# First feed-forward's slots: the low half of the second weight by a transfer inside SBUF instead of a GpSimd copy

## The chip, the cores and the metric

One core of a Trainium2 chip runs the whole program. The metric is the device time of one execution in microseconds (us); before the change it is 1437.46 us, the median of 3 runs (1436.73 to 1438.28). Engine names: PE is TensorE (PEld its weight loader), DVE is VectorE, ACT is ScalarE, POOL is GpSimd, SP is SyncE, which here only issues DMAs.

## The reference, cut to what matters

The program is four residual blocks on x of 16 x 256 tokens by 128: an attention, a feed-forward with experts, a second attention, a second feed-forward. The change is in the first feed-forward. Each token takes a shared expert and the 2 best of 8 experts (hidden width 512), weighted by a softmax over the two gate values:

```python
shared = silu(x_flat @ shared_w1.T) @ shared_w2.T
gate_logits = x_flat @ gate_w.T
top_k_gates, top_k_idx = jax.lax.top_k(gate_logits, TOP_K)
...
h = jnp.einsum('td,ehd->teh', x_flat, experts_w1)
expert_out = jnp.einsum('teh,edh->ted', jax.nn.silu(h), experts_w2)
selected = jnp.einsum('ted,te->td', expert_out, gates)
```

## The kernel before, in words

`first_ffn` does the shared expert for all tokens in 8 blocks of 512 and then the chosen experts in **39 slots** (`SLOTS`) of 256 tokens (`SLOT_T`). Tokens were scattered by expert into the DRAM table `xs`, each expert's stretch filled up to whole slots. So each slot has one expert, whose number is known only at run time: `table` holds, for each slot, the column at which that expert's weights begin.

Products are done in fp32r with each operand split in a high and a low part, hi·hi + hi·lo + lo·hi. A slot therefore needs four pieces of weights of 128 x 512 (256 KB each): high and low of w1, high and low of w2. They are copied into `ring`, which has two halves, used by even and odd slots. GpSimd makes all four copies: `take_w1` (L2199 high, rounded from w; L2200 low, from the table `w1l`) and `take_w2` (L2207 high, from w; L2210 low, from the table `w2l`). It reads the slot's column into a register with `value_load` first. `w2l` is filled beforehand by VectorE (`split_w2`, L2058), counted on `w_lo`.

The order on each engine is written out by hand, with semaphores between them. In round n:
- TensorE: turns x of slot n+1 into `ps_x` (`slot_in`), turns y of slot n-3 into `ps_t` (`slot_out`), `slot_up(n)` (L1846 to L1848, 12 products), `slot_down(n-1)` (L1860 to L1862, 12 products into the single `ps_y`; it waits for `w2_ready`, for `y_done` of the slot before and for `sl_done`).
- ScalarE: `xh` of slot n+1 (L1923), `yout` of slot n-3 from `ps_t` (L1969; `yout` has two buffers, so it waits for the store of two slots earlier, `stored`), then silu of slot n in two halves (L1929, into `s`), then its high part `sh` in two halves (L1980).
- VectorE: `xl` (L2109), the low part `sl` of slot n in two halves (L2143, `s` minus `sh`), then `yb`, the copy of `ps_y` of slot n-1 (L2135, signals `y_done`).
- GpSimd: w1 of slot n+1 once `slot_up(n-1)` is done, then w2 of slot n once `slot_down(n-2)` is done (`y_full`).
- SP, one queue in order: the load of x for slot n+4 into the three buffers of `xin` (L1757; waits until `slot_in(n+1)` is done, reads the slot's row into a register at L1756), then the store of slot n-3 from `yout` to `ys` (L1769; waits for L1969).

Of the kernel before, what the change touches and what calls it, by code (L numbers as in the profile page):

```python
# [16 lines left out]
F32 = mybir.dt.float32  # L17
# [22 lines left out]
SLOTS = (2 * B * S + EXPERTS * (SLOT_T - 1)) // SLOT_T  # L40
# [33 lines left out]
def wait(eng, sem, value):  # L74

    if not isinstance(value, int) or value > 0:
        eng.wait_ge(sem, value)
# [109 lines left out]
def scatter(nc, Z, rt, tile, xs, scattered, choices=(0, 1)):  # L187

    for k in choices:
        nc.gpsimd.indirect_dma_start(xs, bass.IndirectOffsetOnAxis(rt["at"][:, k, tile:tile + 1], 0),  # L190
                                     Z[:, tile * D:(tile + 1) * D], None).then_inc(scattered, 16)
# [1386 lines left out]
NT = B * S // TOK  # L1578
# [68 lines left out]
def first_ffn(nc, X, Z, ident, a):  # L1647
# [3 lines left out]
    E = 8  # L1651
    HC = 4
    HID = HC * P
# [11 lines left out]
    with ExitStack() as ctx:  # L1665
        def sb(name, shape, dt=F32):
            return ctx.enter_context(nc.sbuf_tensor("f0_" + name, shape, dt))
# [4 lines left out]
        def sem(name):  # L1672
            return ctx.enter_context(nc.semaphore("f0_" + name))
# [5 lines left out]
        ring = sb("ring", [P, 2, 4 * HID], F32R)  # L1679
# [12 lines left out]
        table, row_of = sb("table", [P, SLOTS], I32), sb("row_of", [P, SLOTS], I32)  # L1692
        pad_at = sb("pad_at", [P, EXPERTS], I32)
        w2l = sb("w2l", [P, E * HID], F32R)
# [23 lines left out]
        w_hi, w_lo, cast = sem("w_hi"), sem("w_lo"), sem("cast")  # L1718
        up_full, silu_done, sh_done, sl_done = sem("up_full"), sem("silu_done"), sem("sh_done"), sem("sl_done")
        y_half, y_full, y_done = sem("y_half"), sem("y_full"), sem("y_done")  # L1720
        t_full, t_done = sem("t_full"), sem("t_done")
        xin_loaded = [sem(f"xin_loaded{n}") for n in range(AHEAD)]
        stored = [sem(f"stored{n}") for n in range(2)]
        w1_ready, w2_ready = sem("w1_ready"), sem("w2_ready")
        block = ctx.enter_context(nc.Block(no_gpsimd_drain=True))

        def part(c2):
# [8 lines left out]
        w1h_at, w1l_at, w2h_at, w2l_at = [slice(n * HID, (n + 1) * HID) for n in range(4)]  # L1736

        @block.sync
        def _(sp):
            sp.wait_ge(zeroed, 1)  # L1740
            for n in range(SPARE):
                at = E * REGION + n * SLOT_T
                sp.dma_start(a["xs"][at:at + SLOT_T, :].rearrange("(t p) d -> p t d", p=P),
                             zero[:, :, :]).then_inc(padded, 16)
            sp.wait_ge(tables, TABLE)
            for e in range(E):
                at = nc.sync.value_load(pad_at[0:1, e:e + 1], min_val=e * REGION, max_val=e * REGION + B * S)
                sp.dma_start(a["xs"][bass.ds(at, SLOT_T), :].rearrange("(t p) d -> p t d", p=P),
                             zero[:, :, :]).then_inc(padded, 16)
            sp.wait_ge(padded, 16 * (SPARE + E))  # L1750
            sp.wait_ge(scattered, 16 * 2 * TILES)

            def load(n):
                if n >= AHEAD:
                    sp.wait_ge(x_full, NT + n - AHEAD + 1)
                at = nc.sync.value_load(row_of[0:1, n:n + 1], min_val=0, max_val=E * REGION + (SPARE - 1) * SLOT_T)  # L1756
                sp.dma_start(xin[:, n % AHEAD, :, :],  # L1757
                             a["xs"][bass.ds(at, SLOT_T), :].rearrange("(t p) d -> p t d", p=P)
                             ).then_inc(xin_loaded[n % AHEAD], 16)

            for n in range(AHEAD):
                load(n)
            for n in range(-1, SLOTS + BACK):
                if AHEAD <= n + AHEAD + 1 < SLOTS:
                    load(n + AHEAD + 1)
                if 0 <= n - BACK:
                    m = n - BACK
                    sp.wait_ge(t_done, NT + m + 1)
                    sp.dma_start(a["ys"][m * SLOT_T:(m + 1) * SLOT_T, :].rearrange("(t p) d -> p t d", p=P),  # L1769
                                 yout[:, m % 2, :, :]).then_inc(stored[m % 2], 16)  # L1770
            for n in range(2):
                sp.wait_ge(stored[n], 16 * ((SLOTS + 1 - n) // 2))

        @block.tensor
        def _(pe):
# [74 lines left out]

            def slot_down(n):
                pe.wait_ge(w2_ready, n + 1)
                wait(pe, y_done, NT + n)
                for c in range(HC):
                    if c % 2 == 0:
                        pe.wait_ge(sl_done, SHARED + 2 * n + c // 2 + 1)
                    hi, lo = [ring[:, n % 2, w.start + c * P:w.start + (c + 1) * P] for w in (w2h_at, w2l_at)]
                    o = n % 2 * 4 * SLOT_T + c * SLOT_T
                    cols, dst = slice(o, o + SLOT_T), ps_y[:, 0:SLOT_T]
                    nc.tensor.matmul(dst, hi, sh[:, cols], start=c == 0, stop=False)  # L1860
                    nc.tensor.matmul(dst, hi, sl[:, cols], start=False, stop=False)
                    last = nc.tensor.matmul(dst, lo, sh[:, cols], start=False, stop=c == HC - 1)  # L1862
                last.then_inc(y_full, 1)
# [292 lines left out]
        @block.gpsimd  # L2156
        def _(pool):
            nc.gpsimd.memset(zero[:, :, :], 0.0).then_inc(zeroed, 1)
            nc.gpsimd.memset(half[:, :], -0.5).then_inc(late_pool, 1)

            def rstd(n):

                pool.wait_ge(late_step, (LATE_Y_STATS, LATE_X_STATS)[n])
                nc.gpsimd.tensor_scalar(ve_late[:, :], mv_late[:, :, 1], EPS, None, ALU.add).then_inc(late_pool, 1)
                pool.wait_ge(late_pool, LATE_VE[n])
                nc.gpsimd.tensor_tensor(rs_late[:, :], ve_late[:, :], half[:, :], ALU.pow).then_inc(late_pool, 1)

            pool.wait_ge(scattered, EARLY)
            first = GROUPS[-2][0] * TPB
            scatter(nc, Z, rt, first, a["xs"], scattered, (0,))  # L2170
            rstd(0)
            scatter(nc, Z, rt, first, a["xs"], scattered, (1,))
            rstd(1)
            for i in range(first + 1, GROUPS[-1][0] * TPB):
                scatter(nc, Z, rt, i, a["xs"], scattered)
            def cast_into(n, w):
                nc.gpsimd.tensor_copy(w2l[:, n * HID:(n + 1) * HID], w[:, (n + 1) * HID:(n + 2) * HID]
                                      ).then_inc(cast, 1)

            for n in range(E):  # L2180
                cast_into(n, a["w1"])
            pool.wait_ge(routed, AT)
            for i in range(GROUPS[-1][0] * TPB, TILES):
                scatter(nc, Z, rt, i, a["xs"], scattered)
            for n in range(E):
                pool.wait_ge(w_lo, 2 + n + 1)
                cast_into(n, a["w2"])

            def expert_of(n):
                return nc.gpsimd.value_load(table[0:1, n:n + 1], min_val=0, max_val=(E - 1) * HID)  # L2190

            def take_w1(n, at):
                if n == 0:
                    pool.wait_ge(w_lo, 2 + E)
                elif n == 1:
                    pool.wait_ge(up_full, SHARED)
                else:
                    pool.wait_ge(up_full, SHARED + 2 * (n - 1))
                nc.gpsimd.tensor_copy(ring[:, n % 2, w1h_at], a["w1"][:, HID:][:, bass.ds(at, HID)])  # L2199
                nc.gpsimd.tensor_copy(ring[:, n % 2, w1l_at], w1l[:, bass.ds(at, HID)]).then_inc(w1_ready, 1)  # L2200

            def take_w2(n, at):
                if n == 1:
                    pool.wait_ge(y_full, NT)
                elif n > 1:
                    pool.wait_ge(y_full, NT + n - 1)
                nc.gpsimd.tensor_copy(ring[:, n % 2, w2h_at], a["w2"][:, HID:][:, bass.ds(at, HID)])  # L2207
                if n == 0:
                    pool.wait_ge(w_lo, 2 + 2 * E)
                nc.gpsimd.tensor_copy(ring[:, n % 2, w2l_at], w2l[:, bass.ds(at, HID)]).then_inc(w2_ready, 1)  # L2210

            pool.wait_ge(tables, TABLE)
            at = expert_of(0)
            take_w1(0, at)
            for n in range(SLOTS):
                if n + 1 < SLOTS:
                    after = expert_of(n + 1)
                    take_w1(n + 1, after)
                take_w2(n, at)
                at = after  # L2220
# [517 lines left out]
```

## Time and profile before

| what | value |
| --- | --- |
| median of 3 runs | 1437.46 us (1436.73 to 1438.28) |
| profiled execution | 1439.35 us |
| its span, first to last instruction | 1437.6 us |
| mean granted TensorE clock | 0.962 of full speed |
| PE busy | 1299.2 us (90%) |
| DVE busy | 1086.6 us (76%) |
| ACT busy | 971.9 us (68%) |
| POOL busy | 745.1 us (52%) |
| the slots | from about 583 to 715 us of the span |
| L2210, the copy that the change removes | 39 times, 612 to 1071 ns, median 617 |

Busy times are of the one profiled execution. A matmul's end is modelled, so PE's busy time says that the engine had work, not that it ran at its peak. Idle time of an engine matters only where something on the path to the end waits for it. In the rows below, a bracket such as [1.59 <-ACT f_sh L1980] says how long the engine had been idle before the instruction and what ended that; "issue" means that nothing in the profile explains it.

### The profile page before, as it was taken

Reading aid. Unit: us, or ns where it says so; the run is one execution under the profiler, and the core shown is the slowest. Engines: PE = TensorE matmul, PEld = TensorE weight load, DVE = VectorE, ACT = ScalarE, POOL = GpSimd, SP = SyncE. Lnnn points to the kernel's source line nnn. Section 1 sums busy time; section 2 is a strip of 40 time slices with the busy share of each in tenths; the row PEclk is TensorE's granted clock in tenths of the full one; section 3 lists DMA queues with packets and bytes.
Section 4 is the critical chain, followed back from the end, with each engine's and each line's share of the span. In section 5 each row is a group of like instructions: output and inputs, shape, how many; then the busy total and the mean of one; then the engine's idle time right before and its main releaser. Section 6 shows DMA issues by size and latency. Waiting matters only on the chain. (4 is left out here: it accounts for less than half of the span.)

```text
span 1437.6 us, 34171 instructions
## 1 busy us (share of the span) xinstructions
PE 1299.2 (90%) x12121; PEld 989.2 (69%) x12121; DVE 1086.6 (76%) x3011; ACT 971.9 (68%) x1499; POOL 745.1 (52%) x981
## 2 busy tenths in 40 slices
PE   2899999999999779999828999999999998799996
PEld 2456666666665467899826777777777776688886
DVE  5578888888877669566567898889888776476776
ACT  1588888888888546888714777777777777344341
POOL 4776666688764365788575554555454330101112
PEclk9799999999999889999958999999999999899999
DMA  6000000111111110222222111111111110225253
GB/s 238 17 23 20 22 21 20 26 31 31 29 31 46 36 60 27 64 74 79 60 80 59 49 48 48 47 47 48 48 47 39 40 40 17 60 61 133 67 133 82
DMA packets 84429, 77.20 MB, mean 54 GB/s; under 512 B 18224, under 2 KB 72240, under 8 KB 83888
## 3 DMA queue, kind: packets, MB, share of 16 engines
q1 hardware_dynamic: 80176, 66.73, 17.5%
q0 software_dynamic: 4096, 8.40, 2.0%
q8 instruction: 95, 1.56, 0.5%
q14 instruction: 62, 0.51, 0.1%
HBM read 36.26 MB, written 13.63 MB: 35 GB/s over the span
## 5 line engine op out<-in xcount | busy, mean ns | idle before, releaser
L545 ACT ACTIVATE a_p<-a_ps_s 128x1024 f32<-128x1024 f32 x256 | 258.3, 1030 | 21.9 <-PE a_ps_s L404 21.5
L1318 DVE TENSOR_REDUCE a_qt<-a_ps_d 128x2 fp32r<-128x512 f32 x256 | 174.9, 690 | 43.3 <-PE a_ps_d L1097 37.6
L655 DVE TENSOR_REDUCE a_qt<-a_ps_d 128x2 fp32r<-128x512 f32 x256 | 174.6, 688 | 39.9 <-PE a_ps_d L415 38.2
L827 POOL TENSOR_TENSOR a_rn<-a_ss,a_half 128x16 f32<-128x16 f32 x56 | 162.9, 2925 | 1.3
L1219 ACT ACTIVATE a_pg<-a_ps_s 128x1024 f32<-128x1024 f32 x128 | 125.8, 1024 | 24.1 <-PE a_ps_s L1086 22.5
L422 PE MATMUL a_ps_o<-a_p,a_v 128*32 128x256 f32 x2048 | 127.4, 388 | 3.8 <-ACT a_p L545 3.8
L1097 PE MATMUL a_ps_d<-a_kpad,a_qs 128*128 128x512 f32 x256 | 126.9, 499 | 3.6 <-DVE a_qt L1318 1.2
L415 PE MATMUL a_ps_d<-a_kpad,a_qs 128*128 128x512 f32 x256 | 126.7, 495 | 1.9 <-DVE a_qt L655 1.4
L2419 ACT ACTIVATE f_s<-f_ps_g 128x512 f32<-128x512 f32 x72 | 43.0, 599 | 99.2 <-PE f_ps_g L2355 99.0
L1506 POOL DMA_INDIRECT a_picked<-ys,rows x64 | 67.3, 1052 | 61.5 <-PE a_ps_d L1097 50.6
L2143 DVE TENSOR_TENSOR f_sl<-f_s,f_sh 128x512 fp32r<-128x512 f32 x78 | 59.3, 799 | 51.3 <-ACT f_sh L1980 51.2
L422 PEld LDWEIGHTS a_ps_o<-a_p,a_v 128*32 128x32 f32 x2048 | 60.4, 110 | 52.0 <-issue 20.6
L190 POOL DMA_INDIRECT xs<-Z,r_at x64 | 70.1, 1095 | 21.3 <-issue 15.2
L1075 PE MATMUL a_ps_a<-ident,a_qt 128*128 128x128 f32 x512 | 77.8, 275 | 1.4 <-ACT a_kc L1237 0.8
L1241 ACT CAST a_qsm<-a_ps_a 128x512 fp32r<-128x512 f32 x64 | 37.6, 587 | 58.1 <-PE a_ps_a L1075 58.1
L415 PEld LDWEIGHTS a_ps_d<-a_kpad,a_qs 128*128 128x128 f32 x256 | 48.2, 188 | 37.8 <-issue 10.7
L2512 DVE TENSOR_TENSOR f_h<-f_s,f_ps_u 128x512 f32<-128x512 f32 x72 | 48.7, 685 | 33.6 <-PE f_ps_y L2340 19.6
L2340 PEld LDWEIGHTS f_ps_y<-wd,f_p 128*128 128x128 f32 x512 | 63.8, 191 | 10.3 <-DVE f_p L2499 7.2
L2340 PE MATMUL f_ps_y<-wd,f_p 128*128 128x128 f32 x512 | 67.4, 278 | 3.3 <-DVE f_p L2499 2.8
L1147 PE MATMUL a_ps_o<-a_pg,a_v 128*32 128x256 f32 x1024 | 68.5, 385 | 0.4 <-ACT a_pw L1245 0.4
L1097 PEld LDWEIGHTS a_ps_d<-a_kpad,a_qs 128*128 128x128 f32 x256 | 48.5, 191 | 29.0 <-issue 11.4
L1245 ACT ACTIVATE a_pw<-a_ps_s 128x1024 f32<-128x1024 f32 x64 | 65.9, 1030 | 0.1
(385 smaller groups left out, 3790.8 us busy)
## 6 DMA issues: line engine op xcount, KB each, us to landing
a_kpad<-a_kc SPq DMA_DIRECT2D x512, 32.0 KB
f_gb<-spread SPq DMA_DIRECT2D x64, 256.0 KB, 5.6
a_kpad<-a_kq SPq DMA_DIRECT2D x256, 32.0 KB, 1.8
f_xin<-xs SPq DMA_DIRECT2D x39, 128.0 KB, 2.1
ys<-f_yout SPq DMA_DIRECT2D x39, 128.0 KB, 2.1
w<-in_w SPq DMA_DIRECT2D x2, 2304.0 KB, 11.3
out_x<-X SPq DMA_DIRECT2D x8, 256.0 KB, 6.6
xs<-f_zero SPq DMA_DIRECT2D x15, 128.0 KB, 1.9
```

Of the source, the lines that this page charges most:

```text
L190: nc.gpsimd.indirect_dma_start(xs, bass.IndirectOffsetOnAxis(rt["at"][:, k, tile:tile + 1], 0), Z[:, tile * D:(tile + 1) * D], None).then_ ...
L415: nc.tensor.matmul(bank(st.k, f"m{part}")[:, :], qs2[:, (st.k - 1) % 2, t * P:(t + 1) * P], kpad[:, u % PAD_RING, 2 * c:2 * c + 2, :].rear ...
L422: last = nc.tensor.matmul(ps_o[SLOT * j:SLOT * (j + 1), half * S:(half + 1) * S], v32[:, u % V_RING, t, j, :], probs[:, u % 2, j, t, :], s ...
L545: nc.scalar.activation(probs[:, u % 2, 2 * c:2 * c + 2, :, :].rearrange("p a b c -> p (a b c)"), ps_s[:, 2 * c:2 * c + 2, :].rearrange("p ...
L655: nc.vector.tensor_reduce(qt2[:, (k - PEAK) % 4, 2 * part:2 * part + 2, SHIFT], bank(k, f"m{part}")[:, :].rearrange("p (a b) -> p a b", b= ...
L827: nc.gpsimd.tensor_tensor(rn[:, part * c:(part + 1) * c], ss[:, part * c:(part + 1) * c], half[:, 0:c], ALU.pow).then_inc(rn_ready, 1)
L1075: last = nc.tensor.transpose(ps_a[:, n:n + P], stacked(src[:, (u // NG) % 2, kind, t * H + t0:t * H + t0 + G, :]), ident[:, :])
L1097: nc.tensor.matmul(bank(k, f"m{part}")[:, :], qs[:, k % 2, t * P:(t + 1) * P], kpad[:, k % PAD_RING, GLOBAL, 2 * c:2 * c + 2, :].rearrange ...
L1147: nc.tensor.matmul(ps_o[SLOT * j:SLOT * (j + 1), 0:S], v32[:, u % V_RING, t, j, :], pg[:, u % 2, j, t, :], start=t == 0, stop=t == TPB - 1)
L1219: nc.scalar.activation(pg[:, u % 2, 2 * c:2 * c + 2, :, :].rearrange("p a b c -> p (a b c)"), ps_s[:, 2 * c:2 * c + 2, :].rearrange("p a b ...
L1318: nc.vector.tensor_reduce(qt[:, b % 2, GLOBAL, n:n + 2, SHIFT], bank(k, f"m{part}")[:, :].rearrange("p (j s) -> p j s", s=S), AX.X, ALU.ma ...
L2340: last = nc.tensor.matmul(ps_y[:, t * D:(t + 1) * D], src, a["wd"][:, q * D:(q + 1) * D], start=q == 0 and t == 0, stop=q == NQ - 1 and t ...
```

## The change

One of the four pieces changes hands, the low part of w2: the copy L2210 is gone from GpSimd, and SP issues a DMA from `w2l` to `ring` for each slot, inside SBUF, with the column read into a register of SP. `w2_ready` is now signalled by the copy of the high part, and TensorE waits for the transfer as well, on a pair of semaphores used in turn. In SP's loop the new step stands ahead of the load and the store. For slot 0 it waits until `w2l` is complete, for slot n until `slot_down(n-2)` is done, as the GpSimd copy did.

```diff
+        w2l_loaded = [sem(f"w2l_loaded{n}") for n in range(2)]
...
+            def low_w2(n):
+                if n == 0:
+                    sp.wait_ge(w_lo, 2 + 2 * E)
+                else:
+                    sp.wait_ge(y_full, NT + n - 1)
+                at = nc.sync.value_load(table[0:1, n:n + 1], min_val=0, max_val=(E - 1) * HID)
+                sp.dma_start(ring[:, n % 2, w2l_at].bitcast(F32), w2l[:, bass.ds(at, HID)].bitcast(F32)
+                             ).then_inc(w2l_loaded[n % 2], 16)
+
             for n in range(AHEAD):
                 load(n)
             for n in range(-1, SLOTS + BACK):
+                if n + 1 < SLOTS:
+                    low_w2(n + 1)
                 if AHEAD <= n + AHEAD + 1 < SLOTS:
                     load(n + AHEAD + 1)
                 if 0 <= n - BACK:
...
             def slot_down(n):
                 pe.wait_ge(w2_ready, n + 1)
+                pe.wait_ge(w2l_loaded[n % 2], 16 * (n // 2 + 1))
...
-                nc.gpsimd.tensor_copy(ring[:, n % 2, w2h_at], a["w2"][:, HID:][:, bass.ds(at, HID)])
-                if n == 0:
-                    pool.wait_ge(w_lo, 2 + 2 * E)
-                nc.gpsimd.tensor_copy(ring[:, n % 2, w2l_at], w2l[:, bass.ds(at, HID)]).then_inc(w2_ready, 1)
+                nc.gpsimd.tensor_copy(ring[:, n % 2, w2h_at], a["w2"][:, HID:][:, bass.ds(at, HID)]
+                                      ).then_inc(w2_ready, 1)
```

## Rows read from the trace of the kernel before

**Rows 1.** Windows, mid-slots: stretch, length, PE PEld DVE ACT POOL busy, PEclk, DMA share, GB/s.

```profile
620.00:640.00 20.00, 19.90 (x165) 19.38 (x164) 12.77 (x24) 16.69 (x36) 16.77 (x24) 1.00 0.28 81
```

**Rows 2.** Waits, 565 to 720 us: waiter, what ended it, total us, times, longest.

```profile
PEld f_ps_y L1860 <- issue: 6.8, 20, 1.6
```

**Rows 3.** Timeline of PEld, starts of rounds and of `slot_down`: start us, duration us.

```profile
621.30 0.24 PEld L1778 LDWEIGHTS f_ps_x<-ident,f_xin 128*128 128x128 f32 x2
...
623.44 0.19 PEld L1860 LDWEIGHTS f_ps_y<-f_sh,f_ring 128*128 128x128 f32 x1 [0.20 <-issue]
...
624.88 0.24 PEld L1778 LDWEIGHTS f_ps_x<-ident,f_xin 128*128 128x128 f32 x2
...
626.73 0.19 PEld L1860 LDWEIGHTS f_ps_y<-f_sh,f_ring 128*128 128x128 f32 x1
...
628.19 0.24 PEld L1778 LDWEIGHTS f_ps_x<-ident,f_xin 128*128 128x128 f32 x2
```

**Rows 4.** Timeline of DVE in the same two rounds.

```profile
621.30 0.71 DVE L2143 TENSOR_TENSOR f_sl<-f_s,f_sh 128x512 fp32r<-128x512 f32 x1 [1.59 <-ACT f_sh L1980]
621.94 1.09 DVE L2143 TENSOR_TENSOR f_sl<-f_s,f_sh 128x512 fp32r<-128x512 f32 x1
622.96 0.41 DVE L2135 COPY f_yb<-f_ps_y 128x256 f32<-128x256 f32 x1
...
624.62 0.71 DVE L2143 TENSOR_TENSOR f_sl<-f_s,f_sh 128x512 fp32r<-128x512 f32 x1 [0.92 <-ACT f_sh L1980]
...
625.85 0.41 DVE L2135 COPY f_yb<-f_ps_y 128x256 f32<-128x256 f32 x1
```

**Rows 5.** Timeline of POOL, the copies of w2 in the same rounds.

```profile
621.73 0.77 POOL L2207 CAST f_ring<-w 128x512 fp32r x1 [0.25 <-PE f_ps_y L1862]
622.44 1.07 POOL L2210 CAST f_ring<-f_w2l 128x512 fp32r x1
...
625.30 1.11 POOL L2207 CAST f_ring<-w 128x512 fp32r x1 [0.51 <-PE f_ps_y L1862]
```

**Rows 6.** Timeline of ACT in the same rounds.

```profile
621.82 0.37 ACT L1923 CAST f_xh<-f_ps_x 128x256 fp32r<-128x256 f32 x1
622.09 0.38 ACT L1969 COPY f_yout<-f_ps_t 128x256 f32<-128x256 f32 x1
622.76 0.60 ACT L1929 ACTIVATE f_s<-f_ps_u 128x512 f32<-128x512 f32 x1 [0.29 <-PE f_ps_u L1848]
623.48 0.60 ACT L1929 ACTIVATE f_s<-f_ps_u 128x512 f32<-128x512 f32 x1
...
625.40 0.37 ACT L1923 CAST f_xh<-f_ps_x 128x256 fp32r<-128x256 f32 x1 [0.29 <-PE f_ps_x L1778]
```

**Rows 7.** Timeline of SP's queue: the first loads back to back, then mid-slots.

```profile
549.83 0.41 SPq L1757 DMA_DIRECT2D f_xin<-xs  x1
551.01 0.39 SPq L1757 DMA_DIRECT2D f_xin<-xs  x1
...
622.51 0.38 SPq L1757 DMA_DIRECT2D f_xin<-xs  x1
622.94 0.47 SPq L1769 DMA_DIRECT2D ys<-f_yout  x1
...
626.09 0.38 SPq L1757 DMA_DIRECT2D f_xin<-xs  x1
```

**Rows 8.** DMA issues (count, KB each, us to landing); then L1769's landings, and L1051's issues in ns.

```profile
f_gb<-spread SPq DMA_DIRECT2D x64, 256.0 KB, 5.6
ys<-f_yout SPq DMA_DIRECT2D x39, 128.0 KB, 2.1
X<-in_x SPq DMA_DIRECT2D x1, 256.0 KB, 2.8
...
DMA to landing us min/median/max: 1.8/2.1/4.1
...
L1051 SPq DMA_DIRECT2D a_kpad<-a_kc x512: 507/591/1687, 753.1 to 1198.6; - x171
```

## The prediction

> **What bounds the kernel now.** I first cut out the stretch in which the 39 slots run, because the change touches nothing outside it. In that view TensorE is busy 19.90 of 20 us at the full granted clock, GpSimd 16.77 and the DMA engines 0.28 of their time [rows 1]. So nothing on GpSimd or in a queue can save more than TensorE's few idle moments. The waits of the stretch say how few: TensorE's weight loader stood 6.8 us in front of L1860, the first product of `slot_down`, 20 times [rows 2]. That is the ceiling of any gain here.
>
> Next I read two rounds instruction by instruction. A round n of TensorE is: turn x of slot n+1, turn y of slot n-3, `slot_up(n)`, `slot_down(n-1)`. I call its start T. Rounds start at 621.30, 624.88 and 628.19 [rows 3]: one of 3.58, one of 3.31 us, and so in turn, 3.445 in the mean. The long one holds the gap at L1860 (0.20 us idle), the short one has none [rows 3]. TensorE is itself the bound in the short one.
>
> The long round is made by VectorE. The first half of `sl` starts at T+0.00 and takes 0.71, the second takes 1.09, then ps_y is copied to yb, 622.96 + 0.41 = 623.37, and TensorE goes on at 623.44 [rows 3, 4]. In the short round `sl` starts at T-0.26 and yb starts 1.23 us after it instead of 1.66 [rows 4]. The missing 0.43 us is GpSimd's: its copy of the **high** half of w2 (L2207) starts at 621.73, between the two halves of `sl`, and holds `sl`'s second half up until it ends at 622.50. The copy of the **low** half (L2210), which the change takes away, comes after that. It is the one that is held: 1.07 us, from 622.44 to 623.51, while VectorE runs [rows 5]. L2207 always starts 0.42 to 0.43 us after T, when the last `slot_down` is seen done, and after idle time of GpSimd [rows 5]; it is not late because of L2210.
>
> **The change part by part.**
>
> *39 copies L2210 leave GpSimd.* Some 0.6 us each when alone, 1.07 when held. They sit on no path: GpSimd idles 0.25 to 0.51 us before each L2207 as it is. w2 of slot n is copied from T of round n and needed in round n+1, and what gives way to whom stays (L2207 against the second `sl`). I take 0. Bounds: 0, or, if L2210 after all is what VectorE loses to, all long rounds become 3.31 (first rival).
>
> The Trainium skill (SBUF — State Buffer, section "Who interferes with whom") says that a VectorE instruction with two SBUF inputs and a GpSimd instruction that reads SBUF shut each other out for the whole instruction. The trace agrees (1.09 beside 0.71, 1.07 for the held copy); read alone, the rule speaks for this change, since a third less GpSimd reading should mean fewer clashes. Who starts first says which clash goes, and that one costs VectorE nothing.
>
> *One more wait on TensorE in `slot_down`.* It stands beside three others that are already passed in short rounds without a gap [rows 3], so 0 if the data is there. The transfer is issued at T+1.12 (below). It moves 256 KB from 128 rows of 2 KB; X's first load has that size and landed in 2.8 us, `f_gb`, of that size too but issued eight in a row, in 5.6 [rows 8]. With 2.8 it lands at T+3.9. `slot_down` of that slot starts in the next round, at T+3.445+1.85 = T+5.3 at the earliest. Slack 1.4 us; I take 0. If 5.6 it is 1.4 late, the third rival.
>
> *The SP queue.* This is where I expect the cost. SP runs in order. Now, in one pass, it waits for x turned, reads a register, issues a load of x, and issues a store of y four slots back: the load at T+1.21, the store 0.43 later [rows 7]. In front of both the change puts a wait for `slot_down(n-1)`, that is for the end of the round, then a register read and a transfer. So the load and store queued behind it move into the next round:
> - the end is seen at T+0.43 (where L2207 starts) [rows 5];
> - from seeing a semaphore to a DMA whose address is read: ScalarE sees x turned at 625.40, SP's load starts at 626.09: 0.69 [rows 6, 7];
> - to the next DMA with an address, nothing awaited: 549.83 to 551.01, 1.18 [rows 7]. That holds an issue of 0.41; SBUF-to-SBUF issues of the attention took 0.51 to 0.59 [rows 8]. I add 0.10 (nearest the shorter);
> - to the store: 0.43; to its landing: 2.1 [rows 7, 8]; from a released wait to the waiter's start 0.07 (623.37 to 623.44).
>
> The sum, call it S, is 0.43 + 0.69 + 1.18 + 0.10 + 0.43 + 2.1 + 0.07 = **5.0 us** after T. SP is then busy some 3.3 of 3.4 us at most and is no bound itself. The load is late by a round and more (lands near T+4.5) and is wanted two rounds on, at T+6.9: nothing.
>
> The store is another matter. `yout` has two buffers, so ScalarE's copy L1969 of two slots later waits for it. That copy ran at T'+0.79 of the next round (622.09) [rows 6], that is T+4.24. Now it would start at T+5.0, 0.76 late. Behind it on ScalarE wait the slot's silu, `sh`, hence `sl`, yb and `slot_down`. Some of it is absorbed. Silu starts at T'+1.46 and its second half 0.72 later, at TensorE's pace [rows 6]. When late, silu follows the copy by 0.28 (0.38 less the 0.1 by which ScalarE's instructions overlap: 621.82 + 0.37 against 622.09), its second half follows by 0.50, and `sl` 1.14 after that (623.48 to 624.62) [rows 4, 6]. So `sl` starts at T' + S - P + 1.92, P the length of the round before, against T'+3.32 now. It is late only where S - P is over 1.40: after short rounds from S = 4.71, after long ones from 4.98.
>
> From `sl` with the clash to the end of its `slot_down` are 624.88 - 621.30 = 3.58 us. Three rounds can therefore not be shorter than S + 1.92 + 3.58 = S + 5.50, where they are now 10.335. They meet at S = 4.84. With S = 5.0: 10.50 / 3 = 3.50 a round, 0.055 more. Stores 0 to 34 have a transfer ahead of them, so 35 rounds: **+1.9 us**. Bounds: this store's shortest landing, 1.8 [rows 8], and no extra issue give S = 4.6, below the meeting point, 0; a landing of 2.8 as X's and 0.18 of issue give S = 5.8, 11.3 / 3 = 3.77 and +11 us. I stay near the rows of this very store.
>
> *The first slots.* SP now waits for the last split of w2 (w_lo, near 575) before load 3, which went at 571; slot 3 is turned near 583.9. Load and transfer are in by 580. Nothing. After slot 38 the queue is as before.
>
> **Sum.** Profiled execution 1439.35 (span 1437.6) + 1.9 = 1441.3; the same on the median of the runs, 1437.46, gives 1439.4, which I predict.
>
> **The rivals.**
> 1. *Faster: the port.* If L2210 is what costs VectorE its 0.43, or if the moved phases let the second `sl` slip in ahead of L2207, long rounds fall to 3.31: 0.135 x 36 = 4.9 us, 1432.6. For it: the two engines do clash twice in each long round. Against: the order in rows 4 and 5. It decides at one row: `sl` all near 0.7.
> 2. *Slower: the store behind the transfer.* The mechanism that I reckon with, but large. At S = 5.08 it passes 0.2% (2.9 us); S = 5.3 gives 10.80 / 3 = 3.60, 0.155 x 35 = 5.4 us, 1442.9; S = 5.5 gives 7.8. For it: three DMAs inside 2 us where there were two, and every unknown term can only add. Against: the transfer's bytes should be through before the store's begin, and SP has nothing else to do.
> 3. *Much slower: the transfer itself.* Landing in 5.6 us means `slot_down` at T+6.8 and the end 1.44 later, two rounds in 8.2: 4.1 a round, 0.68 x 35 = 24 us, 1461. For it only the `f_gb` row, which is of transfers issued eight in a row.
> 4. *Nothing at all:* S under 4.84, 1437.5. The same outcome as my forecast in what can be measured.
>
> **How the numbers follow.** A measurement of this kernel can tell about 0.2%, 2.9 us, from no change. The case of small or no loss (my forecast with rival 4, from 1437 to 1440.3) gets 0.46, rival 2 0.37, rival 3 0.04, rival 1 0.13. So faster 0.13, same 0.46, slower 0.41. The range goes from 1434.5, which takes in a half-sized gain but leaves the full one out, to 1446.5, S of 5.6.
>
> **What would show it.** Right: SP's load starts near T+2.4 and the store near T+2.9; L1969 has idle time before it that a DMA of `ys` ends; rounds of about 3.5 us, none of them a row of 3.31s; L2207 alone still stretches one `sl` to 1.09; the loader's idle time before L1860 rises from 6.8 us to 8 or 9; L1860 never waits for the transfer. Wrong: `sl` all near 0.7 (rival 1), L1969 without a wait (no cost at SP), or TensorE waiting on the new semaphore (rival 3).

## The result, and the profile after

The changed kernel takes 1448.05 us (median of 4 runs, 1445.64 to 1450.45), the kernel before 1437.49 in the runs beside it. The ratio is 1.0071 (95% interval 1.0053 to 1.0090): 8 to 13 us slower, where I had forecast 1.9 us and a range that ended at 1446.5. The profiled execution is the slowest of the four, 1450.45 with a span of 1448.6.

I first asked in which stage the time went. The weight loads of `slot_down` run from their first to their last start in 131.2 us before (582.1 to 713.3) and in 141.6 after:

```profile
L1873 PEld LDWEIGHTS f_ps_y<-f_sh,f_ring x156: 186/192/192, 582.5 to 724.1; 128*128 128x128 f32 x156
```

That 10.4 us is nearly all of the 11.0 by which the spans differ. In the view of windows, at the same full clock [rows 1], TensorE is busy 18.00 of 20 us instead of 19.90, and the DMA engines move 146 GB/s instead of 81:

```profile
620.00:640.00 20.00, 18.00 (x149) 17.48 (x148) 11.70 (x22) 14.42 (x33) 10.90 (x17) 1.00 0.44 146
```

The waits of the stage (565 to 730 us; waiter, what ended it, total, times, longest) name what grew. The first was not there before at all; the second had 6.8 us [rows 2], the third 1.2:

```profile
ACT f_yout L1982 <- DMA ys<-f_yout: 20.3, 18, 2.3
...
PEld f_ps_y L1873 <- issue: 16.9, 23, 1.6
...
PE f_ps_y L1873 <- DVE f_yb L2148: 11.4, 22, 1.4
```

The first is the wait for the store that the prediction reckoned with. A round and a half of the timeline shows it. Here a round starts at 620.05 (the weight load), SP's transfer goes at 621.15, the load at 622.41, the store at 622.84:

```profile
620.05 0.24 PEld L1790 LDWEIGHTS f_ps_x<-ident,f_xin 128*128 128x128 f32 x2
...
623.77 0.24 PEld L1790 LDWEIGHTS f_ps_x<-ident,f_xin 128*128 128x128 f32 x2
```

```profile
621.15 0.50 SPq L1768 DMA_DIRECT2D f_ring<-f_w2l  x1
622.41 0.39 SPq L1758 DMA_DIRECT2D f_xin<-xs  x1
622.84 0.47 SPq L1781 DMA_DIRECT2D ys<-f_yout  x1
```

```profile
621.59 0.37 ACT L1982 COPY f_yout<-f_ps_t 128x256 f32<-128x256 f32 x1 [0.64 <-DMA ys<-f_yout]
...
626.77 0.37 ACT L1982 COPY f_yout<-f_ps_t 128x256 f32<-128x256 f32 x1 [2.11 <-DMA ys<-f_yout]
```

So the store leaves 2.79 us after the round's start, as worked out (2.83). But this one lands 3.9 us later, not 2.1, and ScalarE's copy, due at 624.56 (0.79 after 623.77), starts at 626.77. The copy one round earlier hangs on the store of 619.37, which landed in 2.1 us; it waited only 0.64. The same view of two stores, the first of the changed kernel, the second of the kernel **before**, where nobody waited for it:

```profile
L1781 SPq DMA_DIRECT2D ys<-f_yout x1: 467/467/467, 622.8 to 622.8; - x1
DMA to landing us min/median/max: 3.9/3.9/3.9
```

```profile
L1769 SPq DMA_DIRECT2D ys<-f_yout x1: 470/470/470, 633.4 to 633.4; - x1
DMA to landing us min/median/max: 4.1/4.1/4.1
```

Store by store, six of the 39 took 3.5 to 4.1 us before (those of 592.1, 633.4, 654.0, 667.8, 681.6 and 695.4); after, ten took 2.8 to 4.3. The long landings are not new. What is new is that they are waited for.

Each of these ten holds up one copy of ScalarE, by 1.3 to 2.3 us, 16.9 of the 20.3 us in all. All other waits, behind landings of 2.0 to 2.6 us, are 0.65 or less. TensorE's rounds say the same. After the first three, which are as before, they are of 3.31 and 3.72 us, one of 3.78, and ten of 4.0 to 5.1; nine of these ten come right after a round with one of the ten long waits, and the tenth is the round of such a wait itself. None of them follows a shorter wait alone. The round after the copy at 626.77 takes 4.87:

```profile
627.09 0.24 PEld L1790 LDWEIGHTS f_ps_x<-ident,f_xin 128*128 128x128 f32 x2
...
631.96 0.24 PEld L1790 LDWEIGHTS f_ps_x<-ident,f_xin 128*128 128x128 f32 x2
```

### The profile page after: what moved, and what is told of

It reads as the page before. It is cut to its first block and busy times, and to the rows that moved or that the text cites. A ratio compares the mean times of both kernels' runs of the same rounds, so it can differ in the third digit from the quotient of the medians.

```text
span 1448.6 us, 34327 instructions
## 1 busy us (share of the span) xinstructions
PE 1300.3 (90%) x12121; PEld 989.6 (68%) x12121; DVE 1086.5 (75%) x3011; ACT 968.4 (67%) x1499; POOL 709.3 (49%) x942
## 5 line engine op out<-in xcount | busy, mean ns | idle before, releaser
L1097 PE MATMUL a_ps_d<-a_kpad,a_qs 128*128 128x512 f32 x256 | 126.9, 498 | 3.5 <-DVE a_qt L1318 1.2
L415 PEld LDWEIGHTS a_ps_d<-a_kpad,a_qs 128*128 128x128 f32 x256 | 48.2, 188 | 37.7 <-issue 10.6
L2351 PEld LDWEIGHTS f_ps_y<-wd,f_p 128*128 128x128 f32 x512 | 63.8, 191 | 10.6 <-DVE f_p L2510 7.6
```

Of the source, the lines that this page charges most:

```text
L415: nc.tensor.matmul(bank(st.k, f"m{part}")[:, :], qs2[:, (st.k - 1) % 2, t * P:(t + 1) * P], kpad[:, u % PAD_RING, 2 * c:2 * c + 2, :].rear ...
L1097: nc.tensor.matmul(bank(k, f"m{part}")[:, :], qs[:, k % 2, t * P:(t + 1) * P], kpad[:, k % PAD_RING, GLOBAL, 2 * c:2 * c + 2, :].rearrange ...
L2351: last = nc.tensor.matmul(ps_y[:, t * D:(t + 1) * D], src, a["wd"][:, q * D:(q + 1) * D], start=q == 0 and t == 0, stop=q == NQ - 1 and t ...
```

## The experiments

Two theories came out of this. Q: the time is the late store, through its long landings. D: the transfers themselves, their bytes or TensorE's further wait. P is the faster rival of the prediction, the port. "Slots" below is the stretch between the first and the last start of the loads of `slot_down` in the profile.

| kernel | median us | ratio to before, 95% | slots us |
| --- | --- | --- | --- |
| before | 1437.49 | 1 | 131.2 |
| changed | 1448.05 | 1.0071 (1.0053 to 1.0090) | 141.6 |
| e1 transfer last in SP's pass | 1443.47 | 1.0037 (1.0023 to 1.0051) | 134.4 |
| e2 three yout buffers | 1442.83 | 1.0035 (1.0021 to 1.0048) | 134.0 |
| e3 no low copy at all | 1438.52 | 1.0009 (0.9999 to 1.0019) | 131.2 |
| e4 only the wait on SP | 1437.65 | 0.9999 (0.9990 to 1.0008) | 132.1 |
| f1 before, one more wait | 1443.08 | 1.0034 (1.0021 to 1.0047) | 134.4 |
| f2 e1, wait moved | 1439.13 | 1.0004 (0.9996 to 1.0013) | 133.0 |
| f3 f2, high copy later | 1435.66 | 0.9970 (0.9958 to 0.9982) | 126.9 |
| f4 changed, wait moved | 1444.16 | 1.0043 (1.0029 to 1.0057) | 138.3 |
| g1 before, copies later | 1438.67 | 1.0003 (0.9995 to 1.0012) | 133.2 |
| g2 e2, wait moved | 1439.62 | 1.0011 (1.0003 to 1.0020) | 131.3 |
| g3 f3 once more | 1435.54 | 0.9980 (0.9972 to 0.9989) | 127.0 |

The kernel before ran beside each group with medians of 1438.1 to 1438.3. The two measures do not agree to better than 2 us: "slots" is of one execution, and what is left of the span outside them went from 1301.4 (e3) to 1308.3 us (g1) from profile to profile. So sizes are given both ways where they matter.

**e1, the transfer behind load and store.**

```diff
             for n in range(-1, SLOTS + BACK):
-                if n + 1 < SLOTS:
-                    low_w2(n + 1)
...
                                  yout[:, m % 2, :, :]).then_inc(stored[m % 2], 16)
+                if n + 1 < SLOTS:
+                    low_w2(n + 1)
```

> The changed kernel with one edit: in SP's pass the transfer of w2's low half stands behind the load and the store instead of ahead of them. Same transfers, same bytes, same extra wait on TensorE, GpSimd as light as in the changed kernel. Theory Q (the store stands in the queue behind the wait for the round's end, its landing varies from 2.0 to 4.3 us, and the yout copy two slots later has no slack left for it): the store of slot n-3 is again issued in the round in which its y was turned, some 2.8 us after the start, and must land 4.2 us after the next start; that is about 2.8 us of slack beyond a landing of 2.1, so even a landing of 4.3 is covered. Time as the kernel before, 1437.5 us within 1.5; L1969's copy never waits for a DMA. Theory D (the transfers themselves, their bytes and the third wait on TensorE, cost the time): stays near 1448. Theory P (the port freed by the missing copy was worth something and the queue hid it): 1432.6.

**e2, one buffer more.**

```diff
-        yout = sb("yout", [P, 2, TPB, D])
+        yout = sb("yout", [P, 3, TPB, D])
...
-                    wait(act, stored[m % 2], 16 * (m // 2))
+                    wait(act, stored[m % 3], 16 * (m // 3))
```

> The changed kernel with yout of three buffers instead of two, nothing else; SP's order stays as changed. Theory Q: the copy into yout waits for the store of three slots back, a whole round (3.4 us) more of slack than now, which covers the longest landing seen (4.3 against 2.1). Time 1437.5 to 1438.5 us, no idle time of ScalarE that a DMA of ys ends. Theory D (transfers or TensorE's new wait): stays near 1448. A mix would lie between.

Both took ScalarE's wait for `ys` away altogether and both gave back 7.2 to 7.6 us of the slots, but neither reached the kernel before: 3 us of the slots were left (5 us by the medians), against theory Q alone. The long rounds are 3.72 us instead of 3.58. In e2, VectorE's yb ends at 623.81 and TensorE goes on at 624.03, 0.22 later; before it was 0.07 (623.37 to 623.44) [rows 3, 4]:

```profile
621.74 0.24 PEld L1790 LDWEIGHTS f_ps_x<-ident,f_xin 128*128 128x128 f32 x2
...
624.03 0.19 PEld L1873 LDWEIGHTS f_ps_y<-f_sh,f_ring 128*128 128x128 f32 x1 [0.36 <-issue]
...
625.46 0.24 PEld L1790 LDWEIGHTS f_ps_x<-ident,f_xin 128*128 128x128 f32 x2
```

```profile
623.40 0.41 DVE L2148 COPY f_yb<-f_ps_y 128x256 f32<-128x256 f32 x1
```

**e3, the copy of the low half left out** (from slot 2 on; the products read stale low halves).

```diff
+                if n < 2:
...
+                else:
+                    nc.gpsimd.tensor_copy(ring[:, n % 2, w2h_at], a["w2"][:, HID:][:, bass.ds(at, HID)]
+                                          ).then_inc(w2_ready, 1)
```

> The kernel before with GpSimd's copy of w2's low half left out from slot 2 on, and nothing in its place (the products read what slots 0 and 1 left there, so the output is not the reference's). It tells what freeing GpSimd is worth by itself. Theory Q holds that the copy of the HIGH half is what holds up the second sl, so 1437.5 us within 1, long rounds still 3.58 with an sl of 1.09 us. Theory P (the low half's copy costs VectorE its 0.43 us): all rounds 3.31, 1432.6 us.

As theory Q had it: the slots take the same 131.2 us, rounds alternate as before, and the longest `sl` is still 1.09. Freeing GpSimd of 37 copies was worth nothing:

```profile
L2143 DVE TENSOR_TENSOR f_sl<-f_s,f_sh x78: 677/715/1093, 579.4 to 709.4; 128x512 fp32r<-128x512 f32 x78
```

**e4, only the wait on SP**, in the kernel before.

```diff
             for n in range(-1, SLOTS + BACK):
+                if 0 <= n < SLOTS - 1:
+                    sp.wait_ge(y_full, NT + n)
                 if AHEAD <= n + AHEAD + 1 < SLOTS:
```

> The kernel before with only the wait for the round's end added to SP's pass, ahead of load and store; no transfer, no register read of the table, GpSimd's copies as before. The store moves from 1.64 us after a round's start to about 1.55 us after the NEXT round's start, against 2.79 in the changed kernel. Theory Q: with a landing of 2.1 it is in time (3.7 against 4.2), so only the long landings (six of 39 stores took 3.5 to 4.1 us in the kernel before, all unseen) now cost, some 0.5 to 0.8 us each after ScalarE's cushion: 1438.5 to 1441.5 us. Theory D (transfers): 1437.5.

A miss: no loss that can be measured. In its profile only two stores were waited for, 1.9 us together, and the slots grew by 0.9. Those were the two stores that landed late while a copy hung on them (3.9 and 3.3 us); the others landed in time, in 2.0 to 2.3 us nearly all. So long landings are waited for here too, there were only fewer of them. The wait alone makes no loss with landings of 2.1 us; that it would make none with ten long ones isn't shown.

**f1, a fourth wait in front of `slot_down`**, in the kernel before, for something long done. Theory W: the wait itself.

```diff
                 pe.wait_ge(w2_ready, n + 1)
+                pe.wait_ge(w1_ready, n + 1)
                 wait(pe, y_done, NT + n)
```

> The kernel before with one line more: in slot_down TensorE also waits for w1_ready of the same slot, which slot_up has long passed; it stands between the waits for w2_ready and for y_done, where the change puts its new one. No transfer, SP and GpSimd as before. Theory W (a further wait, though already met, lengthens TensorE's wake-up after yb by 0.15 us in every long round: 0.22 us from yb's end to the first weight load where it was 0.07): 18 to 19 rounds of 3.72 instead of 3.58, +2.7 us, 1440.5 to 1441 on this chip's 1438. Theory D (what is left in the two last kernels comes from the transfers' bytes): 1438, nothing changes.

The loss is here, with no transfer at all: 3.2 us in the slots, as expected, and 4.8 us (3.0 to 6.8) in the medians, which is more than expected. The long round shown is 3.73 us (635.66 to 639.39), and from yb's end (637.31 + 0.41) to the load are 0.23:

```profile
635.66 0.24 PEld L1778 LDWEIGHTS f_ps_x<-ident,f_xin 128*128 128x128 f32 x2
...
637.95 0.19 PEld L1861 LDWEIGHTS f_ps_y<-f_sh,f_ring 128*128 128x128 f32 x1 [0.36 <-POOL f_ring L2211]
...
639.39 0.24 PEld L1778 LDWEIGHTS f_ps_x<-ident,f_xin 128*128 128x128 f32 x2
```

```profile
637.31 0.41 DVE L2136 COPY f_yb<-f_ps_y 128x256 f32<-128x256 f32 x1
```

```profile
L1856 PEldq EVENT_SEMAPHORE  x39: 51/943/1358, 582.0 to 711.3; - x39
```

With four waits it is never held, and from 583 to 715 us the queue has 111 others of line 77 (the helper `wait`) where it had 75. The 36 new ones, one per slot, wait for `y_done`, with L1857 and the load still to be issued behind it: in the round shown yb ends at 637.72, the new one starts at 637.76, L1857 at 637.88, the load at 637.95. First row the kernel before, then f1:

```profile
L77 PEldq EVENT_SEMAPHORE  x75: 51/51/51, 583.4 to 714.7; - x75
```

```profile
L77 PEldq EVENT_SEMAPHORE  x111: 51/51/51, 584.4 to 714.9; - x111
...
L1857 PEldq EVENT_SEMAPHORE  x39: 51/51/51, 581.3 to 714.7; - x39
```

The changed kernel has the same pattern, its L1869 lasting 51 ns each time.

**f2, f4 and g2, the wait moved into `slot_up`,** where TensorE is not held: f2 on e1, f4 on the changed kernel, g2 on e2.

```diff
             def slot_up(n):
...
+                    if h == 1 and n > 0:
+                        pe.wait_ge(w2l_loaded[(n - 1) % 2], 16 * ((n - 1) // 2 + 1))
...
             def slot_down(n):
                 pe.wait_ge(w2_ready, n + 1)
-                pe.wait_ge(w2l_loaded[n % 2], 16 * (n // 2 + 1))
+                if n == SLOTS - 1:
+                    pe.wait_ge(w2l_loaded[n % 2], 16 * (n // 2 + 1))
```

> The kernel with the transfer last in SP's pass, and TensorE's wait for the transfer moved out of slot_down into the middle of the slot_up before it (ahead of the second half's products, where TensorE is not held by anything). Transfers as in the changed kernel, landing some 3.4 us after a round's start, against 4.6 for the moved wait. Theory W with the queue theory: both costs are gone, rounds 3.58 and 3.31 in turn, 1438 us as before. Theory D: stays at 1441 to 1443.

> The changed kernel with SP's order as changed (transfer ahead of load and store) and only TensorE's wait for the transfer moved into the slot_up before. Theory: the wake-up term of some 2.7 us goes, the store's lateness stays. That leaves 1438 + 7 to 8 = 1445 to 1446.5 on this chip. If the two terms do not add (late stores already make the rounds in which the wake-up matters): 1447 to 1448.

> The changed kernel, SP's order as changed (transfer first), with both repairs: yout of three buffers and TensorE's wait moved into the slot_up before. If the late store and the fourth wait are the whole loss, this is the kernel before again: rounds of 3.58 and 3.31 in turn, 1438 to 1439.5 us. If the transfers' bytes or SP's later loads cost anything by themselves, it stays at 1441 or above.

f2 is the kernel before again (ratio 1.0004; 1.3 us of its 133.0 in the slots are one wait for a transfer, which before the move would have had 0.7 us more). f4 gives back 3.3 us of the slots and leaves ScalarE's wait at 20.4 us, so the two terms add. Its median is a little under the expectation, with runs from 1442 to 1449. In g2 the slots take 131.3 us, so 39 transfers of 256 KB cost nothing there by themselves. Its median is 1.4 us (0.4 to 2.9) above that of the kernel before, just over what was expected; its profile does not show where, and that stays open.

**f3 and g1, the copies of w2 after both `sl`.** f3 is f2 with this edit, g3 the same kernel again, g1 the kernel before with it (and so without the transfer).

```diff
                 elif n > 1:
                     pool.wait_ge(y_full, NT + n - 1)
+                    pool.wait_ge(sl_done, SHARED + 2 * n)
```

> As the last one, and GpSimd's copy of w2's high half waits until both halves of sl of the slot before are made, so that it can no longer come between them. With only that copy left there, GpSimd ends its work of the round some 3.5 us after the round's start. If the clash of the high half's copy with the second sl is all that makes the long rounds long: every round 3.31, about 35 x 0.135 = 4.7 us under the kernel before, 1433.4 on this chip. If something else comes last instead (the w1 copies now reaching into the next sl): between 1434 and 1438.

> The kernel before (all four pieces copied by GpSimd) with only this edit: both copies of w2 wait until both halves of sl of the slot before are made. Does the faster kernel need the transfer? With both copies there, GpSimd's work of a round starts 1.36 us after its start and is 4 x 0.56, some 2.4 us with the starts: it ends near 3.8 us, half a us into the next round, on top of the next first sl, which starts at 0.01. If that clash replaces the old one: rounds of 3.4 to 3.6, 1437 to 1440 us. If the copies slip past each other without holding sl: 3.31 a round as with the transfer, 1433 to 1435.5.

> The fastest kernel so far once more (transfer last in SP's pass, wait moved into slot_up, high half's copy after both sl), beside the one without the transfer: 1434 to 1436.5 us, every round 3.31.

f3 beats both kernels: 0.3% and, measured again, 0.2% under the kernel before. After the first three rounds, each of f3 is 3.31 us, but for two of 3.36 and 3.37, and the slots are 4.3 us shorter. The ratio says as much (2.6 to 6.0 us), but the nine runs go from 1430.8 to 1437.4, and the medians of f3 and g3 are only 2.6 us under the kernel before (for f3 I had expected 1433.4). TensorE has no idle moment in the window:

```profile
620.00:640.00 20.00, 20.00 (x171) 20.00 (x170) 12.24 (x24) 17.31 (x37) 10.80 (x19) 1.00 0.49 160
```

In g1 GpSimd's four copies do not fit between two `sl`. Its last one, L2200, clashes with the next round's first `sl`, which starts at 626.28 and takes 0.84, and nearly every round is 3.50 to 3.52 us. The slots come out 2.0 us longer; the median doesn't move (0.5 us, -0.7 to 1.7):

```profile
625.97 0.62 POOL L2199 CAST f_ring<-w 128x512 fp32r x1
626.52 1.07 POOL L2200 CAST f_ring<-f_w1l 128x512 fp32r x1
```

So the transfer is what makes room for the late copy. That is the change's use, which it did not draw by itself.

## Why the prediction was wrong

The sign was right and the size was not: 1.9 us forecast, some 10.5 measured, beyond the range. The bounds that stand beside the sum, up to S = 5.8 and 11 us, did take it in, but the range was ended at S = 5.6; and that bound fits by luck, for it stands for one even lateness and has no wake-up in it.

- *What bounds, and GpSimd's copy: right.* The high half's copy makes the long rounds (f3), the low half's is worth 0 (e3). Rival 1 is refuted as a gain of this change; most of its 4.9 us is real (4.3 us in f3's slots, 2.6 by its median) and needed another edit. What I read out of the rule on the port was also too large: one GpSimd copy in four goes, not a third of its reading.
- *The SP queue: right in place and order.* The transfer went at T+1.10, the load at T+2.36, the store at T+2.79 (1.12, 2.40, 2.83 worked out). SP's issue of it took 0.50.
- *The store's landing: the mis-sized term.* "To its landing: 2.1" is a median. The row beside it said 1.8/2.1/4.1 [rows 8], and I bounded it by 2.8, from another transfer. While the store had 3.9 us to spare, the 4.1 never showed; once S sits at the edge of the slack, the lateness is made by the long ones: 16.9 of ScalarE's 20.3 us of waiting. Of an even loss of 0.055 us a round, the 1.9 us of the sum, the rounds show nothing. I gave this term 1.9 us. The slots say 7.6 by e2 (141.6 - 134.0) and 7.1 by f4 (138.3 - 131.2), the medians 5.9 by either.
- *"One more wait on TensorE: 0": the step that failed.* I argued from the short rounds, where TensorE is not held. In the long ones it is released by yb, and there the fourth wait costs some 0.15 us of wake-up. In the slots that is 3.2 us by f1 (134.4 - 131.2) and 3.3 by f4 (141.6 - 138.3), by the medians 4.8 and 4.7. The slack of the transfer itself was as worked out: it lands in 2.3 us, and the changed kernel has no wait of TensorE for it.
- *Rival 3 did not come about,* rival 2 in part: the late store was the larger loss. That its size is near the S = 5.5 value (7.8 us) is luck. S at a usual landing is the 5.0 worked out (2.79 + 2.1 + 0.07); ten long landings made nearly all of the wait.
- *The signs.* SP's times and the stretched `sl` came as named. The loader's idle time before L1860, now L1873, rose to 16.9 us and not to 8 or 9, and there are no rounds of 3.5 us.

Sum of the measured terms: in the slots 7.6 + 3.2 = 10.8, for 10.4; by the medians 5.9 + 4.8 = 10.7, for 10.6. Neither term alone would have left the range.

## What to carry to other kernels

A DMA's landing has a spread, and an engine waits for its long end as soon as the slack is less than that; ask for the maximum of the very transfer, not the median, and keep more than one round between a store and the reuse of its buffer. Put an awaited step into an in-order queue at the place where its wait ends last, behind what is ready sooner. A met wait is free only where the engine isn't held: count the waits ahead of the instruction that restarts a held engine, and move the ones long met elsewhere.

## What the runs showed of the hardware

Ahead of `slot_down`, two waits went into one semaphore instruction and a third on the weight load; a fourth (f1) made a new instruction and lengthened the wake-up of a held TensorE from 0.07 to 0.23 us. Stores of 128 KB from SBUF to DRAM that usually land in 2.1 us took 3.5 to 4.1 us in six of 39 cases of the kernel before. They are not spread evenly: the last four of the six are every fourth store, 13.8 us apart (654.0, 667.8, 681.6, 695.4), and g1, with rounds of 3.50 us, had none over 2.7. The Trainium skill (DMA: Bandwidth & Descriptors, section "Anatomy of one DMA — SWDGE (gpsimd) path") says, of DMAs that GpSimd issues, that the semaphore waits for the write's receipt, which can be surprisingly long with HBM as the target. The traces here, of DMAs that SP issues, don't show the receipt, and HBM as target can't be the only cause: one transfer that stays inside SBUF took 4.7 us to land too.

```profile
DMA to landing us min/median/max: 2.3/2.3/4.7
```

What delays single ones was not tried.
